# Expert products in plain float32, token-major outputs and expert jobs of two batches, in a two-layer kernel on one core

## The chip, the cores and the metric

The kernel runs on one core of a Trainium2 chip. The metric is device time in microseconds (us) from launch to the last store; lower is better. The core has TensorE (PE: matrix products and 128x128 transposes, results to PSUM), VectorE (DVE), ScalarE (ACT), GpSimd (POOL) and SyncE (SP, which here only issues DMAs). Each engine runs its own instruction list in order. Engines wait for each other through semaphores, so an instruction whose input is late holds up everything behind it on its engine.

## The reference, cut to what matters

The input has 8 batches of 1024 tokens of 128 features, in float32. Four layers follow each other, each on the layer-normalised rows, each added to its input:

```
A: k, q, v = x@Wk, x@Wq, x@Wv ; decay = clip(f(tanh(x@cs1)@cs2))       # linear attention
   state_t = state_{t-1}*decay_t + k_t v_t ; y_t = q_t . state_t ; y @ Wo
B: top 2 of 8 experts, weights renormalised, width 352:
   y = sum_e cw_e * ( silu(x@W1_e) * (x@W3_e) ) @ W2_e
C: conv over 3 tokens, silu, state-space scan with 16 states over t,
   gated by silu(x@Wz), @ Wout + bout
D: top 2 of 8 experts, width 128, and 2 shared experts of width 128 on every token
```

A and C scan over the tokens of a batch. B and D work on rows gathered by expert.

## The kernel before, in words

Letters A to D name the layers as above, `T` = 1024, `HW` = 512 (half a batch), `P` = 128.

**Layer A**, per batch: PE turns the normalised rows (`s_turn`), ACT copies them out of PSUM as float32 and again as float16 (L1115, L1117), DVE makes the remainder as a second float16 (`a_lo`, L1340). For each of 16 steps (8 features by 2 halves) PE makes the value product in three float16 passes (`a_value`, through `product`, L835 to L837), DVE multiplies with k (L1377), scans (L1366), multiplies with q (L1384), and PE adds up through `Wo` with the weights stationary and 512 columns moving (`a_sum`, L885). The result is feature-major: ACT copies it (L1139), PE turns it back (`transpose_out`, L860), DVE adds it to x (L1345).

**Layer C**, per batch: products for u, z, dt and the B and C rows; these rows go to DRAM and come back broadcast to 128 partitions (`c_brow`, `c_crow`, 512 KB each). For each of 16 states ACT makes exp (L1173), DVE multiplies, scans and multiplies (L1435, L1440, L1426), and PE adds up 1024 columns (`c_sum`, L927). Then `c_out` (L937), a copy with the bias on ACT (L1177), transposes, and the addition.

**Layers B and D** go by jobs. A job is one layer of one batch, 16 jobs in all. `prepare` normalises the rows, turns them for the gate's product, chooses the experts (`m_choose`), ranks (`m_rank`) and places them (`m_place`), then POOL scatters the rows to DRAM with indirect DMAs (L796, 16 per job) in blocks of rows of one expert. Rows are held as two float16 parts (L1111, L1331). A job has 12 blocks of 256 rows, each half of 128 rows with its own expert: 192 blocks. Per block SP loads the up weights (`b_w13`), the down weights (`b_w2`) and the rows (`b_rows`). PE turns both parts (L973), ACT copies them (L1202), PE makes the up products in three float16 passes each (L835 to L837: 12 products of 128x128 in a B block, 4 in a D block), ACT makes silu (L1207, L1214), DVE gates (L1540, L1551), PE makes the down product with the weights stationary (L998), so its result is feature-major; ACT copies it to `y_ring` (L1223), PE turns it (L1007), ACT scales it by the gate into `yrow` (L1231), and SP stores it. When a job's blocks are stored POOL gathers the outputs back and adds them to x (L813, 16 indirect DMAs per batch and layer). The shared experts of D run at the head of the D job, also in three float16 passes, with a copy and transposes of the output.

The float16 parts of the expert weights are made on the chip at the start: maxima (`peak`, L1269), a power-of-two scale (`scale`), the split on ACT and DVE (L1074, L1289), and a store to DRAM (`keep`).

The order of all steps is a string, `ORDER`. Each letter takes the next step of one chain (the dictionary `chain`). Every engine goes through the same list and carries out its own part of each step, so the string fixes the order on every engine, on SP's and POOL's queues too.

Of the kernel before, what the change touches and what calls it, by code (L numbers as in the profile page):

```python
# [6 lines left out]
BF16 = mybir.dt.bfloat16  # L7
F16 = mybir.dt.float16
# [6 lines left out]
P = 128  # L15
# [27 lines left out]
class BankUses:  # L43
# [32 lines left out]
    "CWAAAWAAWWAAWAAWAAAPAAAAAAAAAAAAAAAAAAAAosAokqAswokqsAkqwoswqkAwosAokqAswokqAswokqAswokqAswoqAswoqAswoqAswoq"  # L76
    "AswoqAswoqAWWwWWWWWsoqswCqCAwwCAwwwAAPAAPAAAPPAPPAPPAAAPAPAPPAAPPAAPAAAAAPAAPKoPAsqkowesPKAqkwoesAPokqAswokP"
    "qAswokqAswPokqAswokqAPswokqAswoPqAswoqAswPoqAswoqAswoqAswoqARAwRRRRRsAoqAwsqTwwMwwAUwTPAALPUAPVUKAALAAVMNAAe"
    "PTAAAPULUAAVUKMAAYPAALPVAAOZUPAASALRNPePoTYUPMAVPosskAqUKkqOZwoLUPVPAsTSwoRkLUPANeMYOZPSRVUKqLUVwLoUPNeTYMOV"
    "UZPTKsALMskUoSkLqARPswqkqwowVPsANeokqAsYUPowkVAqUKswToPqLUALVwsMNeoqAYsPOZwoUSqAsRwoqAPVwoUKsTLAMVUsNLPqeUoY"  # L80
    "OZqAAwSwRsAVUKTLMqUAVwLoUsNeVUqYOZwKTwLUVMwAwSNwRPAeAYAOPAALPAPAUAAAPVAAUKATALZVUMAASLUARAVOZAANeAAUYALROZVU"
    "oSTLKNsMqkAYPSowPesARPqkUoPwPVUKsALqkUowLVAsNeokqAYswoUkqTAsMwoOZVUKAkLqUoTLsOAZSwMqSGkoRwRsAVkqNeoswAsUYoOZ"
    "VUKAsLUoTLqMASqwRoGwqsAwsqowqGAswoqAswoqGswVqUPPVAGwwNePPwwUwAYTPKOZGMLUSRLPVGAAUPNeYAVUTGCLUKMALAAAAAPAPVAA"
    "AAAAAAAAAAANeCAAYPUOZCoCVUKTAsCPoCqSsCRwCkqCMkLPVCCCPCACCowsCCPqkCCACCNeCoCYsPPAUqkwoLUsAVkwoUKsALCCVkoUCqAs"
    "LCwCoOUqAqwsbbwoTcVAcsZUKkkNMCLTUdSVqRewqxYwbxMdboOZhALSURsNedoqAswoYdOqAswZSOZoRqASVwRoUKsTLUsAqMVLwqUowpyc"
# [12 lines left out]
    "cbxUPPGNVbPeUdTYPMyKLOUGZLRSPAVAPNeUYAPhAOAVUKpTZAMPxyLAVSAUxcNeLhPdUAVRUbhYTbLUKPAOhMZASARVGLAAAAUdpNeVUxYT"
    "AOMcApLbUKhALyZcVASAURxdNeGVUTYALKhOUAZVbMyPpRLSAcpAUdNeAAGVUYKTdoOyZsLqURAxcLSwGkVbMoUdsNeVUqkTYLUKhOAGwZMV"
    "SyoLRdpUscNeGVkUYqOZTxKALUowsARMVLSGyobkqsNekqUYOZhARwPSwVdoUKTsAoLUPqAswLVMqUkkoNeVPsUYOZTPKwLMAkUSLoGVAsUN"  # L100
    "eoVUsYOZKTAqPLUqMVwqRNPoRLsSwYeUpOZAVcURoKTLUqMVAsLUNeoVUqYOZsKTALwxMwVKqNohUYeOZwLRUsRdAeVUTqKwoMwpLAKsyVqN"
    "eoesUYLqbOZVUSRLpSwSVNccxUSGbhLNwVUYxLwwVUKwTLyMwVhOeNUKaNPxTyGpePyhKYLMPVcpGUKPPLVPyPTPMPGpPyPGOCNeUYPNLCKC"
    "GYCOZeCCNeCYOZRVURLaNKVGTYCMOCZUCNLRPYKOZVCPNSSYSOZTGSeCeRPMSTCRUKCPCMLCTVeUCMNLTPCYVMUOZPTCMRLSCVCUKPNLCYVU"
    "OZTCCSNLePCCVYCMCOUKCCZCCLVCCPOZSCSNCCPPbbccYCOZPSNdPPRRYRPPxORbxPPZbhSdRNPePhYTOZPMSGURdpdPcpLcxbxdbhUyPPVT"
    "dPUKMyLPGUTLMPVGxUbPNeVUYOZGTKhMLULVSdNpeUpGYyVRchcOZUKTLUxGyMxRLVSdUbhbNeYVUTGdOpKZLUpyRhLcycMSGVdUxNeVUhYT"
    "LUKOPxMVLbUZhbRNdeVUPTGLpSKpyYVMPUdOcycxLUbxPbhZRNeVUYPThdOKLUpScpyPLVcMUxZRNVdexUTPLUhSbybLKVYUMhOZPSNPdeYO"
    "ZVUKPTLpUpyLPVSMcUxdcNVRbUhKYTLyxUMVRLUheNeVUYTLOpKMZVUxNLKpUYOZVUTRLhSMyccKVULNVKUYLOZVUeLKOZVULpNSpNSSGVUY"
    "eTNLMRVURRNPKOyaPePeyPLePYVeUPPNKTMyPLGVPeCKUPKCPGCCPTCCMCLTGMOYNeCYOZCaSNCGRPeYVUKPOZLOCZTMNVSURPYCCOSCeRCK"
    "CPLCVUTLCKMVZSPCCRCCPNeCCYUCCLVCCPOZTCCNeMCCYURCCLSPVTCOZCCSNRPbbccMCYTUKPMdTPOZMSNLGxxbYOZVbUhSdNRGepyLRhcY"
    "dVpPUcxTdNGPyMbxLbhUTPVpPchyLMYdpPcxUPbOxZPVUKPNPhyLPPKYdVpSORPyPbhcZUSdNePLUPRYOZTSdORVUKMLUxpTbLMVcyxZRdbh"  # L110
    "USGNeVdUpTYLUKOhyZMRNVLexdUxPSVcUYKPOZTLUGNepLYVOZUchbNMePVUYdOhTSyRbKMpGLUycLVRZpUSSdNVexPUTYyLhKUMVOPZbxcL"
    "URNRpdSVUcTKhyGLUeYVLOUbMZVUKTdGNxpLUehyRbLcMVGSYUpdOVUKTyxZLhNbPeUMVYLUSxOZcVUKTPLNMVhUYNSLeUpYePOZVUcyLxKV"
    "OZhUKLUPNVUpYSOZSeyLVSPPeNKUYLpOZKPVULVNGSUPeLeNVURYRLRORVNGRaRNPyTYCMCPTCMUKCTCCMPLVUPeCCLOCKNaPYCOZePPSTVU"
    "CRNMPGLTKYGMOVUZCPCeSRNKPCLPGVUCKTCPCLCKYGMNCCeYCeVeCOZGCCSOUCKCLVZCCNCCPeYGCSCPRCCRNCTYCCOGbbccMCGZUKdOTZMe"
    "LTPRxSSMVURLTxbdNVbUPhMYTLOhPZSMNVpdUKpTPyMxLxccYhdObPybVUZhSLNePYVUKLNdVpYcpydPcxdOybZxSbhNYPOZPdSNeYOZpOSZ"
    "GchySxdRpbPRcxyRGbPPhRRRPPhdPPpdcxyGPPbpTMcPyxTUMbGhPLhdUVUKGLPUpTMxycLVbPpUNeGVPUdTPLycKUMYLGOZRPSVxUNePGYO"
    "ZbVUTKLMVUxNLPehUYOZbVUTKLVdpNPcUhRMyLRehUPSdSVUKTpMPLUcxybxLVYdOpUPVUKTyhLUcZVMRPNheLUYNpSeVUYPTxLOcyZKVMhO"
    "ZURLURNpPeVUYTLOSMyVZSKUpGNLSUYeOZVUKTLyMVNCRSCYRCCeUCGCLCCUCOZCSRCPCCVUTKPCPCCLUCVMCLCCCCUCCVUKCCLVCCNCCKCC"
    "YCCeTCUMCNCeebbccLUCYdOVUKTLxMKVULxZdNhbbKVdUpYdRcOhLyeeZpeOZVUcLRxRNdVSSNxbUSGYhbLOyadVNhUKTNMPpcxyPexbPLbh"
    "GYPPVdpUKhPyLGpcTPxycMbPdOVUKaNGhPLexYdOVbUPKhTGZPNpeYLNcPySPRMGeYTOZMROSZSdRPVGxdbpUKPNLyGYTcOZVUepMNLSTYcV"  # L120
    "UMxOKZTyMhPLbNeYVUOZhSLRNdSPRVURpKYLxNyPcpbYdKTVOyhcMPZKxTUMNdhTYbMOePZLOpeSxycZdSVbhUSPKNYLOpKxyZPdVhcUbNSY"
# [11 lines left out]
def build(nc, t, out):  # L133
# [1494 lines left out]
```

## Time and profile before

| what | value |
|---|---|
| median of 3 runs | 1948.63 us (1947.36 to 1950.04) |
| profiled execution: span from first to last instruction | 1960.7 us (the page gives no other time for it) |
| busy: PE / DVE / ACT / POOL | 76% / 72% / 59% / 51% of the span |
| mean granted TensorE clock | 0.890 of full speed |
| DMA | 393.00 MB, mean 200 GB/s |

Busy time is time in which an engine carried out an instruction that the profiler records. A float32 matmul shows as two instructions. Idle time is put down to what ended it; "issue" is idle time that ended with nothing that the profile shows.

### The profile page before, as it was taken

To read this page: it belongs to the slowest core of one execution; us is meant where nothing else is said; L and a number is where in the kernel's file an instruction comes from. 1 tells how busy PE (TensorE), PEld (TensorE's weight loads), DVE (VectorE), ACT (ScalarE), POOL (GpSimd) and SP (SyncE) were. 2 spreads that over 40 slices of the span, in tenths; PEclk is the share of its full clock that TensorE was granted. 3 is DMA by queue.
4 is the path that set the end of the run, shared out by engine and by line. 5 is a ranking of instruction groups with operands and counts; after the bars stand their busy time and mean duration, and the time that the engine had idled before them with its cause. 6 is when DMAs were issued, how large, how long until landed. Compare 5 with 4: busy or idle time off the path is not lost.

```text
span 1960.7 us, 32118 instructions
## 1 busy us (share of the span) xinstructions
PE 1485.2 (76%) x9858; PEld 950.1 (48%) x9858; DVE 1404.1 (72%) x2696; ACT 1155.1 (59%) x2075; POOL 999.0 (51%) x711
## 2 busy tenths in 40 slices
PE   0767988889997778769887788789768778766761
PEld 0223655555662446656554555466536544433540
DVE  3777869699988886678856774886688399398410
ACT  2232453577466544867357755985866697674550
POOL 0024335602728364748274826356888258655465
PEclk9979999999998798889997988799889899878895
DMA  8931545478928654979657985897789588487563
GB/s 261 136 96 58 146 138 126 108 242 279 271 87 239 188 149 116 295 250 292 191 135 230 284 288 130 264 327 240 199 273 317 173 252 272 110 284 210 135 162 66
DMA packets 343140, 393.00 MB, mean 200 GB/s; under 512 B 37784, under 2 KB 280504, under 8 KB 342712
## 3 DMA queue, kind: packets, MB, share of 16 engines
q1 hardware_dynamic: 297912, 357.23, 59.9%
q0 software_dynamic: 45056, 33.72, 9.6%
q8 instruction: 79, 1.29, 0.3%
q14 instruction: 93, 0.76, 0.1%
HBM read 333.10 MB, written 59.69 MB: 200 GB/s over the span
## 4 chain that ended last, share of the span: by engine, by line
PE 25%; issue 20%; POOL 19%; DVE 15%; ACT 10%; DMA 7%; SPq 3%; POOLq 0%; DVEq 0%; ACTq 0%; another core or an unknown queue 0%
POOL x L813 6%; POOL rows_D L796 6%; POOL rows_B L796 4%; PE bank L998 4%; PE bank L927 3%; DVE arena_a L1366 3%; PE bank L835 2%; PE bank L837 2%; PE bank L836 2%; POOL xrow L794 2%; DVE arena_c L1440 2%; DMA mix<-weights_B 2%; DVE arena_a L1384 2%; PE bank L871 2%; PE bank L885 2%
## 5 line engine op out<-in xcount | busy, mean ns | idle before, releaser
L813 POOL DMA_INDIRECT x<-outs,slot_idx x256 | 501.3, 1958 | 379.2 <-DMA outs<-yrow 301.4
L835 PE MATMUL bank<-xT_ring,mix 128*128 128x128 f16 (+1 forms) x1536 | 296.9, 228 | 57.1 <-DMA mix<-weights_B 17.3
L927 PE MATMUL bank<-arena_c,ident 128*128 128x512 f32 x512 | 285.5, 688 | 47.2 <-DVE arena_c L1426 46.8
L836 PE MATMUL bank<-xT_ring,mix 128*128 128x128 f16 (+1 forms) x1536 | 296.3, 228 | 0.0
L837 PE MATMUL bank<-xT_ring,mix 128*128 128x128 f16 (+1 forms) x1536 | 296.1, 228 | 0.0
L1440 DVE TENSOR_TENSOR_SCAN arena_c<-arena_c 128x1024 f32<-128x1024 f32 x128 | 291.0, 2281 | 3.6 <-ACT arena_c L1173 3.3
L998 PE MATMUL bank<-mix 128*128 128x128 f32 (+1 forms) x1536 | 231.5, 297 | 54.2 <-issue 22.5
L998 PEld LDWEIGHTS bank<-mix 128*128 128x128 f32 (+1 forms) x1536 | 206.4, 206 | 88.7 <-issue 84.2
L796 POOL DMA_INDIRECT rows_D<-xrow,slot_idx x128 | 208.4, 1628 | 74.8 <-POOL xrow L794 35.5
L835 PEld LDWEIGHTS bank<-xT_ring,mix 128*128 128x128 f16 (+1 forms) x1536 | 169.2, 110 | 108.6 <-issue 55.9
L1551 DVE SCALAR_TENSOR_TENSOR mix<-bank,winv,mix 96x256 f32<-96x256 f32 (+1 forms) x192 | 91.4, 476 | 178.6 <-ACT mix L1214 106.1
L796 POOL DMA_INDIRECT rows_B<-xrow,slot_idx x128 | 160.9, 1257 | 76.1 <-POOL xrow L794 35.5
L836 PEld LDWEIGHTS bank<-xT_ring,mix 128*128 128x128 f16 (+1 forms) x1536 | 167.8, 109 | 36.2 <-issue 31.4
L1231 ACT ACTIVATE yrow<-bank,xg 128x128 f32<-128x128 f32 x384 | 120.0, 364 | 107.2 <-PE bank L1007 77.5
L927 PEld LDWEIGHTS bank<-arena_c,ident 128*128 128x128 f32 x512 | 101.1, 216 | 147.3 <-issue 83.0
L837 PEld LDWEIGHTS bank<-xT_ring,mix 128*128 128x128 f16 (+1 forms) x1536 | 168.0, 109 | 0.1
L1426 DVE TENSOR_TENSOR arena_c<-arena_c 128x1024 f32<-128x1024 f32 x128 | 154.5, 1214 | 12.3 <-DMA arena_c<-bc_rows 12.0
L1435 DVE TENSOR_TENSOR arena_c<-arena_c 128x1024 f32<-128x1024 f32 x128 | 154.2, 1214 | 12.7 <-DMA arena_c<-bc_rows 9.4
L1173 ACT ACTIVATE arena_c<-arena_c,A_w 128x1024 f32<-128x1024 f32 x128 | 145.6, 1148 | 27.0 <-DVE arena_c L1440 26.1
L885 PE MATMUL bank<-arena_a,Wo 128*128 128x512 f32 x256 | 140.2, 639 | 27.3 <-DVE arena_a L1384 26.5
L1223 ACT COPY y_ring<-bank 128x256 f32<-128x256 f32 x192 | 71.1, 370 | 144.7 <-PE bank L998 134.4
L1214 ACT ACTIVATE mix<-bank,winv 96x256 f32<-96x256 f32 (+1 forms) x192 | 91.0, 474 | 80.9 <-PE bank L837 65.4
(219 smaller groups left out, 2882.0 us busy)
## 6 DMA issues: line engine op xcount, KB each, us to landing
arena_c<-bc_rows SPq DMA_DIRECT2D x256, 512.0 KB
mix<-weights_B SPq DMA_DIRECT2D x192, 352.0 KB
mix<-weights_B SPq DMA_DIRECT2D x192, 192.0 KB
outs<-yrow SPq DMA_DIRECT2D x192, 128.0 KB
mix<-weights_D SPq DMA_DIRECT2D x192, 128.0 KB
xg<-rows_B SPq DMA_DIRECT2D x96, 129.0 KB
xg<-rows_D SPq DMA_DIRECT2D x96, 129.0 KB
mix<-weights_D SPq DMA_DIRECT2D x192, 64.0 KB
```

What stands on the lines that cost most here:

```text
L796: pool.indirect_dma_start(out=xs_d[s, b % 2], out_offset=bass.IndirectOffsetOnAxis(ap=slot_idx[:, q % RJ, c, j:j + 1], axis=0), in_=xrow[: ...
L813: pool.indirect_dma_start(out=x[:, b % XS, j, :], out_offset=None, in_=y_d[q], in_offset=bass.IndirectOffsetOnAxis(ap=slot_idx[:, q % RJ, ...
L835: pe.matmul(o, hi, xh, start=True, stop=False)
L836: pe.matmul(o, hi, xl, start=False, stop=False)
L837: return pe.matmul(o, lo, xh, start=False, stop=True)
L885: filled(added_up(b, k), pe.matmul(bank[A_BANKS[1]][:], Wo[:, f, :], qs[:, k % RQ, :], start=(f == 0), stop=(f == EF - 1)))
L927: last = pe.matmul(bank[C_BANKS[h]][:], ident[:], half(hb[:, n % RR, :], h), start=(n == 0), stop=(n == NS - 1))
L998: last = pe.matmul(o[:, j * P:(j + 1) * P], w2(q, k, j)[0:rows, c, :], h_ring[n % RH][0:rows, at:at + P], start=(c == 0), stop=(c == NC[s] ...
L1173: act.activation(dA[:, n % RDA, :], dt, ACT.Exp, scale=A_sb[:, n:n + 1]).then_inc(c_dA.sem, 1)
L1426: dve.tensor_tensor(hb[:, n % RR, :], hb[:, n % RR, :], Cb[:, g % RB, :], ALU.mult).then_inc(c_prod.sem, 1)
L1435: dve.tensor_tensor(hb[:, n % RR, :], Bb[:, g % RB, :], w, ALU.mult).then_inc(c_dBx.sem, 1)
L1440: dve.tensor_tensor_scan(hb[:, n % RR, :], dA[:, n % RDA, :], hb[:, n % RR, :], 0.0, ALU.mult, ALU.add).then_inc(c_scan.sem, 1)
```

## The change

1. **Numbers.** The splitting of weights and rows into float16 parts is gone, with `peak`, `scale`, `split`, `keep`, `a_lo`, `m_hi`, `m_rows`, `m_lo`. Rows and weights stay float32, and each product is one float32 matmul in place of three float16 ones. The expert weights are copied DRAM to DRAM at the start.
2. **Token-major outputs.** The down product, the shared down product, `a_sum` and `c_out` take the activations as the stationary operand and the weights as the moving one, 128 columns each. The transposes of outputs and the copies ahead of them are gone (`b_out`, `b_down_read`, `a_end`, `s_end`, `c_out_read`, `sh_out`, `sh_read`); the bias of `c_out` comes from a matmul with one row.
3. **Jobs of two batches.** 9 jobs: B01 B23 D01 B45 D23 B67 D45 D6 D7. A job of two batches has 20 blocks, one of a single batch 12, so there are 164 blocks. A job's choice and placing runs once for both batches. The scatters become a chain of their own (`X`), as do the shared experts (`u`, `l`, `v`, `n`). A gather waits for the gathers of the job before.
4. **Residence.** x has 8 places rather than 7; `xn` is gone, the rows are normalised right into `xrow`; the statistics are kept by parity of the batch.
5. **`ORDER`** is a new string of 4840 letters (before 5769).

```diff
-            def product(o, hi, lo, xh, xl):
-                pe.matmul(o, hi, xh, start=True, stop=False)
-                pe.matmul(o, hi, xl, start=False, stop=False)
-                return pe.matmul(o, lo, xh, start=False, stop=True)
...
-    JOBS = [(j[0], int(j[1])) for j in "B0 B1 B2 D0 B3 B4 D1 B5 D2 B6 D3 B7 D4 D5 D6 D7".split()]
+    JOBS = [(j[0], [int(b) for b in j[1:]]) for j in "B01 B23 D01 B45 D23 B67 D45 D6 D7".split()]
+    BLOCKS = [-(-((2 * T * len(own) + E * (P - 1)) // P) // NBT) for _, own in JOBS]
...
             def a_value(b, k):
-                filled(f"A{b}.v{k}", product(o, Wv[0][:, c], Wv[1][:, c], half(xA_hi, h), half(xA_lo, h)))
+                filled(f"A{b}.v{k}", pe.matmul(fill(f"A{b}.v{k}"), Wv[:, f, :], half(normA, h), start=True, stop=True))
             def a_sum(b, k):
-                filled(added_up(b, k), pe.matmul(bank[A_BANKS[1]][:], Wo[:, f, :], qs[:, k % RQ, :],
-                                                 start=(f == 0), stop=(f == EF - 1)))
+                for j in range(TH):
+                    rows = slice(j * P, (j + 1) * P)
+                    last = pe.matmul(bank[A_BANKS[1]][:, rows], qs[:, k % RQ, rows], Wo[:, f, :], start=(f == 0 and j == 0),
+                                     stop=(f == EF - 1 and j == TH - 1))
...
             def c_out(b, h):
-                filled(n, pe.matmul(fill(n), Wout[:], half(w, h), start=True, stop=True))
+                for j in range(TH):
+                    rows = slice(j * P, (j + 1) * P)
+                    pe.matmul(o[:, rows], ones[0:1, :], bout_row[:], start=True, stop=False)
+                    last = pe.matmul(o[:, rows], half(w, h)[:, rows], Wout[:], start=False, stop=True)
...
             def rows_turned(q, k):
-                for part in range(2):
-                    for i in range(NBT):
-                        c = part * NB + i * P
-                        last = pe.transpose(o[:, c:c + P], xg16[:, m % RX, i, part * D:(part + 1) * D], identh[:])
+                for i in range(NBT):
+                    last = pe.transpose(o[:, i * P:(i + 1) * P], xg[:, m % RX, i, 0:D], ident[:])
             def up_products(q, k, name, parts):
-                        last = product(o[:, i * NB + j * P:i * NB + (j + 1) * P], wd[:, v, f], wd[:, v + 1, f],
-                                       xT_ring[:, m % 2, 0, rows], xT_ring[:, m % 2, 1, rows])
+                        last = pe.matmul(o[:, i * NB + j * P:i * NB + (j + 1) * P], wd[:, v, f], xT_ring[:, m % 2, rows],
+                                         start=True, stop=True)
             def down_product(q, k):
-                        last = pe.matmul(o[:, j * P:(j + 1) * P], w2(q, k, j)[0:rows, c, :], h_ring[n % RH][0:rows, at:at + P],
+                        last = pe.matmul(o[:, j * P:(j + 1) * P], h_ring[n % RH][0:rows, at:at + P], w2(q, k, j)[0:rows, c, :],
                                          start=(c == 0), stop=(c == NC[s] - 1))
-            def outs_turned(q, k):
...
-            def outs_moved(q, k):
...
+            def m_gather(q, i, c, first):
+                s, b = JOBS[q][0], JOBS[q][1][i]
+                if c == 0 and first == 0:
+                    if i == 0:
+                        for r in range(RY):
+                            m = max(m for m in range(block_no[q, BLOCKS[q] - 1] + 1) if m % RY == r)
+                            wt.wait_ge(y_out[r], 16 * (m // RY + 1))
+                    if q:
+                        job_gathered(wt, q - 1)
```

## Rows read from the trace of the kernel before

**Rows 1.** The page: busy time, share of the span and instructions of each engine.

```profile
PE 1485.2 (76%) x9858; PEld 950.1 (48%) x9858; DVE 1404.1 (72%) x2696; ACT 1155.1 (59%) x2075; POOL 999.0 (51%) x711
```

**Rows 2.** The page: shares of the span in the chain that ended last.

```profile
PE 25%; issue 20%; POOL 19%; DVE 15%; ACT 10%; DMA 7%; SPq 3%; POOLq 0%; DVEq 0%; ACTq 0%; another core or an unknown queue 0%
```

**Rows 3.** Busy us by stage: window, length, PE, PEld, DVE, ACT, POOL, clock, DMA share.

```profile
426.00:544.00 118.00, 108.03 (x843) 73.17 (x842) 112.43 (x132) 73.87 (x132) 50.22 (x17) 0.97 0.87 268
1684.00:1821.00 137.00, 95.67 (x456) 53.49 (x454) 102.03 (x163) 92.01 (x145) 81.07 (x49) 0.84 0.70 206
```

**Rows 4.** Timeline of PE, full clock: start us, us, line, operation, count.

```profile
556.25 0.60 PE L946 MATMUL bank<-ident,xn 128*128 128x128 f32 x4
565.51 1.02 PE L902 MATMUL bank<-arena_c,Wconv 128*128 128x512 f32 x2
567.23 0.22 PE L835 MATMUL bank<-xT_ring,mix 128*128 128x128 f16 x1
567.28 0.22 PE L836 MATMUL bank<-xT_ring,mix 128*128 128x128 f16 x1
568.81 1.50 PE L998 MATMUL bank<-mix 128*128 128x128 f32 x12
570.15 0.22 PE L835 MATMUL bank<-xT_ring,mix 128*128 128x128 f16 x1
```

**Rows 5.** Costliest groups of ACT: busy us, mean ns, idle before, releaser.

```profile
L1231 ACT ACTIVATE yrow<-bank,xg 128x128 f32<-128x128 f32 x384 | 120.0, 364 | 107.2 <-PE bank L1007 77.5 <-PE bank L837 12.1 <-remote 5.3
L1202 ACT COPY xT_ring<-bank 128x512 f16<-128x512 f16 x192 | 111.5, 581 | 41.8 <-PE bank L973 36.6 <-remote 2.6 <-PE bank L1007 1.4
L1173 ACT ACT_TABLE_LOAD x80 | 102.6, 1283 | 1.5
L1223 ACT COPY y_ring<-bank 128x256 f32<-128x256 f32 x192 | 71.1, 370 | 144.7 <-PE bank L998 134.4 <-issue 8.6 <-PE bank L1042 0.7
L1139 ACT COPY arena_a<-bank 128x512 f32<-128x512 f32 x16 | 9.4, 586 | 74.8 <-PE bank L885 74.2 <-issue 0.5
L1111 ACT CAST xrow<-xn 128x1024 f16<-128x1024 f32 x16 | 16.9, 1054 | 0.0
```

**Rows 6.** Groups of DVE.

```profile
L1440 DVE TENSOR_TENSOR_SCAN arena_c<-arena_c 128x1024 f32<-128x1024 f32 x128 | 291.0, 2281 | 3.6 <-ACT arena_c L1173 3.3
L1540 DVE SCALAR_TENSOR_TENSOR mix<-bank,winv,mix 128x512 f32<-128x512 f32 x96 | 71.2, 742 | 55.8 <-PE bank L837 38.2 <-issue 4.9 <-ACT mix L1207 4.8
L1331 DVE TENSOR_TENSOR xrow<-xn,xrow 128x1024 f16<-128x1024 f32 x16 | 19.4, 1216 | 14.0 <-ACT xrow L1111 12.2 <-issue 1.8
```

**Rows 7.** The waits: who waited for whom, us in total, times, longest.

```profile
PE bank L853 <- DVE Wv_lo L1289: 42.8, 1, 42.8
PE bank L1007 <- ACT y_ring L1223: 36.6, 41, 5.2
PE bank L998 <- ACT yrow L1231: 20.6, 28, 2.1
PE bank L1007 <- ACT yrow L1231: 12.5, 8, 6.6
```

**Rows 8.** Timeline at the start, and the first statistics of layer C.

```profile
23.70 0.20 ACT L1067 ACTIVATE tanh_base<-cols 128x1 f32<-128x1 f32 x1 [13.07 <-DMA cols<-in_bbc]
50.40 3.59 PE L871 MATMUL bank<-arena_a,cs_w 128*32 128x512 f32 x4 [5.71 <-POOL before L765]
354.80 1.64 DVE L1310 BATCH_NORM_STATS2 stats_C<-x 128x6 f32<-128x128 f32 x8 [3.95 <-DMA x<-outs,slot_idx]
```

**Rows 9.** Timeline of POOL in the last job: scatters from the first row, then gathers.

```profile
1850.45 1.08 POOL L796 DMA_INDIRECT rows_D<-xrow,slot_idx  x1 [0.83 <-POOL xrow L789]
1876.73 1.61 POOL L813 DMA_INDIRECT x<-outs,slot_idx  x1 [0.30 <-issue]
1950.77 1.56 POOL L813 DMA_INDIRECT x<-outs,slot_idx  x1 [0.30 <-issue]
1952.63 1.56 POOL L813 DMA_INDIRECT x<-outs,slot_idx  x1 [0.30 <-issue]
```

More of the change, by code:

```diff
@@ L81 @@
[L81 to L85, printed above, removed]
@@ L402, in attention, with blocks, shared @@
+        def blocks(name):
+            return [(name, q, k) for q in range(len(JOBS)) for k in range(BLOCKS[q])]
+        def shared(name, n):
+            return [(name, b, i) for s, own in JOBS if s == "D" for b in own for i in range(n)]
         def attention(b):
             steps = [(n, "A", b, h) for n in ("s_turn", "s_turned") for h in range(NH)]
-            steps += [(m, b, "cs", h) for m in ("a_in", "a_read") for h in range(NH)] + [("a_lo", b)]
+            steps += [(m, b, "cs", h) for m in ("a_in", "a_read") for h in range(NH)]
@@ new lines, in m_rstd, with m_scatter @@
+            def m_rstd(q, i):
+                inverse_deviation(JOBS[q][0], JOBS[q][1][i])
+            def m_scatter(q, c, first):
+                s = JOBS[q][0]
+                if c == 0 and first == 0:
+                    wt.wait_ge(s_zeroed[s, NTH[q] % ROW_SETS[s]], 16)
+                    wt.wait_ge(placed, q + 1)
+                    all_scattered(wt, q - 1)
+                    pool.tensor_copy(xrow[:, 0:JT[q], D], gate12[:, q % RJ, 0, 0:JT[q]]).then_inc(row_gate, 1)
+                    wt.wait_ge(row_gate, q + sum(JT[:q]) + 1)
+                for j in range(first, first + 2):
@@ L854, in s_turn @@
                 filled(n, last)
-            def transpose_out(s, b, h):
-                U.wait_empty(wt, f"{s}{b}.o{h}")
-                o = fill(f"{s}{b}.outT{h}")
-                for j in range(TH):
-                    last = pe.transpose(o[:, j * P:(j + 1) * P], OUT[s][:, h, j * P:(j + 1) * P], ident[:])
-                filled(f"{s}{b}.outT{h}", last)
             def a_in(b, name, h):
@@ L919, in c_bc @@
                 U.wait_empty(wt, f"C{b}.u{h}")
-                filled(n, pe.matmul(fill(n, rows=BC), Wbc[:, 0:BC], half(xs, h), start=True, stop=True))
+                filled(n, pe.matmul(fill(n, rows=BC), Wbc[:], half(xs, h), start=True, stop=True))
             def c_sum(b, n):
@@ L955, in m_logits @@
                                      start=True, stop=True)
-                filled(f"lg{q}", last)
+                filled(f"lg{q}.{i}", last)
             def m_rank(q):
@@ L1124, in a_in @@
                 if name == "k":
-                    read(n, act.activation(half(kT, h), psum(n), ACT.Copy, scale=down["Wv"]))
+                    read(n, act.copy(half(kT, h), psum(n)))
                 if name == "q":
```

868 lines of the change are left out of this document (354 added, 514 removed).

## The prediction

> **What bounds the kernel now.** I read the page's busy times first, then the chain, then the stages, then the rows of what changes. No engine is full: PE 76%, DVE 72%, ACT 59%, POOL 51% [rows 1]. The chain that ended last is spread in the same way: PE 25%, "issue" 20%, POOL 19%, DVE 15%, ACT 10%, DMA 7% [rows 2]. The reader is to see that nothing here is worth its busy time. Engines alternate, in an order written out by hand, and the span is 475 us longer than PE's busy time. The stages differ [rows 3]: from 426 to 544 PE is busy 108 and DVE 112 of 118 us, so there both are full; from 1684 to 1821, the last scan layer beside a D job, DVE has 102 of 137 us, ACT 92, POOL 81, and the handovers between them fill the rest.
>
> **The change part by part, on PE.** Prices are distances between starts at full clock [rows 4]. Float16 passes start 0.05 to 0.06 us apart; I take 0.056, so a product of three costs 0.168 (512 columns: four times as much, 0.67). Six float32 products of 128 columns, each with its own stationary operand, take 1.34 (568.81 to 570.15), so 0.223 each. A single pass of 0.22 has 0.16 of tail, so a float32 product of 512 columns in 1.02 costs 0.86, and four float32 transposes in 0.60 are 0.11 each.
> - Up products: 96 B blocks of 12 and 96 D blocks of 4 are 1536 at 0.168, 258 us. Afterwards 80 of 12 and 84 of 4, 1296 at 0.223, 289 us: +31.
> - Value and shared up products: 192 of 512 columns, 0.67 to 0.86: +36.
> - Down products: 768 to 648 (6 or 2 per block) at 0.223: -26. `a_sum` and shared down: 160 times 0.86 become 160 times 4 x 0.223: +5. `c_out`: 16 times 0.86 become 16 times 8 x 0.223 with the bias: +15. The one-row bias product stands in no row; it lies between nothing and a full 0.223, and I take the full price.
> - Output transposes, 384 for blocks and 192 others at 0.11: -63. Turns of block rows: 768 at 0.056 become 328 at 0.11: -7.
>
> PE in all: -9 us, so nothing. "Plain float32" doesn't relieve PE; what it gains in fewer blocks and turns it gives back at 0.223 against 0.168.
>
> One rule of the Trainium skill speaks against these edits. The row above shows six different stationary operands in 1.34 us, so their loads stay behind the streaming. The page "TensorE: Matmul & The Clock Gate" (Weight-path perf modes) says that the fast way of loading weights is open to types other than FP32 only; every product of the new kernel would lose it. If a slower load showed at each product the PE sum would turn clearly positive; by the row it adds nothing, and I go by the row.
>
> From rows alone, the bound of the new `a_sum`, whose stationary operand DVE has only just written: below, its four parts cost the 0.86 of now; above, they can't hide their loads behind each other and cost as much as four half-filled 0.60 groups would allow, 4 x 0.38 (0.223 and one tail of 0.16), +0.66 each, 106 us in all. I take 0.223, since the down product has the same form.
>
> **On ACT** [rows 5]. The `y_ring` copies go: -71. The turned rows are 256 float32 columns instead of 512 float16 ones, at the 0.370 of the copy of that shape, 164 times: 111.5 to 61, -51. Casts and half-batch copies that only served the parts and the feature-major outputs go, 17 us (L1111) and some 80 half-batch copies at 0.586, 47 us: -64. Fewer blocks: `yrow` 120 to 103, -17, and 44 silus fewer, at the 0.37 to 0.59 of copies of their shapes, -20. Weight splits -10. Table loads: walking through both order strings and counting the changes between exp, ln and the silu/tanh group on ACT gives 207 before (the trace shows 204) and 173 afterwards, -34 at 1.283: -44. Sum -277 of 1155.
>
> **On DVE** [rows 6]. The three remainders (32 of 1.216) -39. The gates keep their price (the form without a scalar lies between nothing and the 0.742 of now); 16 wide ones and 28 of half the width fewer, -12 for the first and up to as much again for the others: -25. Maxima and splits at the start -20. Choice and placing run 9 times with wider rows, not 16 times: about -25, between nothing and half of their cost. Sum -109 of 1404. The scans (128 of 2.281) stay.
>
> **POOL** keeps its 256 gathers and 256 scatters: 0. **DMA**: 28 of 192 blocks go, 15% of what blocks load and store; the two 512 KB broadcasts per state stay.
>
> **What of it reaches the end.** An engine's saving counts in the share of its busy time that lies on the chain: ACT 10% of 1960.7 is 196 of 1155, 0.17, so -47; DVE 294 of 1404, 0.21, so -23; PE 0.33 of 9, -3; DMA 137 on the chain, half of it blocks' loads, 15% of that: -10. Output turns: PE stood 37 + 21 + 12 = 70 us for the `y_ring` and `yrow` copies [rows 7]; two handovers per block go, but other work shares these gaps, so half, -35. The start: PE waited 42.8 us for the low part of Wv [rows 7] and made its first product at 50.4 [rows 8]. The last small loads are in at 23.7 [rows 8]; normalising and turning needs some 7 more, so 31: -20. The DRAM to DRAM weight copies are hidden by the 150 us of layer A before any expert block; without that cover they cost some tens of us once.
>
> Against this stands the pairing. Sixteen scatter DMAs take 26.3 us (1850.45 to 1876.73), gathers 1.86 each [rows 9]. A pair puts 32 in a row, 53 us, ahead of 20 blocks, and its second batch waits for all of it. At the start the first pair can't begin before batch 1 has left layer A, so C's first statistics stay near 355 [rows 8] in spite of the earlier start. Where the string has other DVE work at hand this costs nothing; for the seven pairs I take +30, between 0 and 7 x 26 = 182. The new wait of a gather for the job before holds POOL's scatters behind it, but POOL does these in order anyway; it is within the 30.
>
> Sum: -47 - 23 - 3 - 10 - 35 - 20 + 30 = -108. The span of 1960.7 becomes 1853. The runs' median lies 12 below the profiled span, so the time is 1841.
>
> **Rivals.**
> 1. PE sets the pace and ACT's and DVE's relief turns into their idle time. For it: PE is first in busy time and on the chain, 108 of 118 us where things are dense, and its work falls by only 9. Against: the last third, where PE has 96 of 137. Only the start and PE's own share come off, 20 and 10 at the clock of now: span 1931, time 1919.
> 2. Slower: lumps on POOL. A pair's 32 scatters, 20 blocks and 32 gathers stand in one piece between two layers, and the scan layers of the next batches run dry. In the string, between the statistics of C4 and C5 stand 44 gather DMAs and 30 scatter DMAs, 44 x 1.86 + 30 x 1.64 = 131 us of POOL at its best, beside some 91 us of DVE; between the same marks the old string has 24 and 32, 97 us, beside some 120 of DVE. It decides from the point where the work in hand is shorter than the 53 us scatter. Each pair then pays 26: 182 in place of the 30, sum +44, span 2005, time 1993. Against: the letters of DVE work between a pair's preparation and its gathers are some 200 us for the later pairs.
>
> **How the numbers follow.** Forecast 0.58, rival 1 0.23, rival 2 0.17; 0.02 for a draw by other ways. The forecast's own range: without lumps and with all 70 us of the turns -173, time 1776; with ACT's and DVE's shares halved and 60 for the lumps -43, time 1906. The range over all reaches below for a chain that gives back more of ACT than its share (some 30 us), 1745, and above to between the rivals, 1960. A measurement tells 0.2%, 4 us, from no change. Faster 0.80 (the forecast and rival 1), same 0.03, slower 0.17.
>
> **What would show it.** ACT near 880 busy, DVE near 1295, PE within 30 of 1485, POOL near 1000. The first product of layer A near 31; the first statistics of C near 355. Float32 products 0.22 apart in the up products and in the new `a_sum`; if 0.38, the load isn't hidden. No idle PE behind copies of outputs. If PE's share rises above 80% with little gain, rival 1; if POOL's share of the chain grows well over 19% and DVE waits for gathers, rival 2. The forecast is wrong if the time is above 1906 or below 1776.

## The result and the profile after

The kernel after takes 2002.57 us (1998.39 to 2009.84, 4 runs), the kernel before beside it 1948.18: ratio 1.027 [1.024 to 1.030], slower by 54 us. The forecast was 1841. Its profiled span is 2003.1 us at a mean granted clock of 0.863 of full speed; before it was 1960.7 at 0.890.

The kernel after, the page: busy time, share of the span and instructions.

```profile
PE 1528.4 (76%) x7536; PEld 1041.4 (52%) x7536; DVE 1302.6 (65%) x2413; ACT 886.6 (44%) x1623; POOL 884.7 (44%) x702
```

Against [rows 1] ACT lost 268 us and DVE 101, PE gained 43, POOL's recorded time fell by 114. ACT's and DVE's work is what was forecast (880 and 1295). PE's isn't (within 30 of 1485 was forecast), nor POOL's (near 1000): POOL has as many scatters and gathers as before, but each is shorter (gathers 1.79 us in place of 1.96, scatters 1.21 in place of 1.44 on average). None of ACT's and DVE's relief is to be seen in the span, which means that it became idle time. PE's idle time is 475 us before and after.

The chain of the profile after breaks off (its engines' shares add up to 11%), so its shares can't be set against [rows 2]; groups, waits and marks have to do. Groups of the kernel after: busy us, mean ns | idle before, releaser.

```profile
L917 PE MATMUL bank<-xT_ring,mix 128*128 128x128 f32 x1952 | 287.5, 300 | 43.6 <-ACT xT_ring L1086 21.7 <-DVE mix L1385 7.0 <-DMA mix<-weights_D 6.2
L859 PE MATMUL bank<-arena_c,ident 128*128 128x512 f32 x512 | 290.1, 702 | 104.3 <-DVE arena_c L1256 104.2
L819 PE MATMUL bank<-Wo,arena_a 128*128 128x128 f32 x1024 | 152.4, 297 | 52.8 <-DVE arena_a L1215 51.5 <-DVE x L1176 1.2
L1106 ACT ACTIVATE yrow<-bank,xg 128x128 f32<-128x128 f32 x328 | 102.1, 363 | 187.0 <-PE bank L930 186.3
L1086 ACT COPY xT_ring<-bank 128x256 f32<-128x256 f32 x164 | 60.3, 368 | 167.3 <-PE bank L905 103.2
```

`yrow` costs 102.1 and the turned rows 60.3, as counted from [rows 5] (103 and 61). What has grown is PE's waiting: 104.2 us for DVE in the sums of layer C (L859) and 51.5 in those of layer A (L819), where the kernel before had 46.8 and 26.5. The timeline of PE (start us, us, line, operation, count):

```profile
10.62 3.08 PE L794 MATMUL bank<-ident,arena_a 128*128 128x128 f32 x8 [10.62 <-POOL blk_no L716]
13.78 3.59 PE L805 MATMUL bank<-arena_a,cs_w 128*32 128x512 f32 x4
256.31 0.41 PE L905 MATMUL bank<-ident,xg 128*128 128x128 f32 x2
541.18 1.95 PE L917 MATMUL bank<-xT_ring,mix 128*128 128x128 f32 x16
550.14 1.13 PE L819 MATMUL bank<-Wo,arena_a 128*128 128x128 f32 x8 [0.36 <-DVE arena_a L1215]
```

Layer A's first product starts at 13.78, not at 50.40 as in [rows 8]: 37 us earlier, where 20 were counted. Eight float32 up products (16 instructions) take 1.95 us and four in the new `a_sum` 1.13. Less the tail of 0.16 that is 0.22 and 0.24 apart; [rows 4] gave 0.22. But no block is worked on before 256.31, and the first statistics of C come at 408.28, where [rows 8] has 354.80:

```profile
408.28 1.64 DVE L1154 BATCH_NORM_STATS2 row_sums<-x 128x6 f32<-128x128 f32 x8
```

So after 37 us of lead at the start the kernel is 53 us behind one fifth of the way, and 42 at the end of the profiled spans (54 by the medians: the profiled execution before was a long one, 12 above its median).

### The profile page after: what moved, and what is told of

Read it like the earlier page. It is cut to its first block and busy times, and to the rows that moved or that the text cites. A ratio compares the mean times of both kernels' runs of the same rounds, so it can differ in the third digit from the quotient of the medians.

```text
span 2003.1 us, 25885 instructions
## 1 busy us (share of the span) xinstructions
PE 1528.4 (76%) x7536; PEld 1041.4 (52%) x7536; DVE 1302.6 (65%) x2413; ACT 886.6 (44%) x1623; POOL 884.7 (44%) x702
## 5 line engine op out<-in xcount | busy, mean ns | idle before, releaser
L917 PE MATMUL bank<-xT_ring,mix 128*128 128x128 f32 (+1 forms) x2592 | 366.7, 295 | 58.1 <-ACT xT_ring L1086 21.7
L917 PEld LDWEIGHTS bank<-xT_ring,mix 128*128 128x128 f32 (+1 forms) x2592 | 340.6, 202 | 100.8 <-issue 64.8
L859 PE MATMUL bank<-arena_c,ident 128*128 128x512 f32 x512 | 290.1, 702 | 104.3 <-DVE arena_c L1256 104.2
L859 PEld LDWEIGHTS bank<-arena_c,ident 128*128 128x128 f32 x512 | 104.6, 223 | 227.2 <-DVE arena_c L1256 133.7
L819 PEld LDWEIGHTS bank<-Wo,arena_a 128*128 128x128 f32 x1024 | 136.7, 206 | 114.6 <-DVE arena_a L1215 93.1
L1385 DVE TENSOR_TENSOR mix<-bank,mix 128x256 f32<-128x256 f32 (+1 forms) x164 | 68.1, 419 | 194.9 <-ACT mix L1098 192.2
L819 PE MATMUL bank<-Wo,arena_a 128*128 128x128 f32 x1024 | 152.4, 297 | 52.8 <-DVE arena_a L1215 51.5
L740 POOL DMA_INDIRECT rows_D<-xrow,slot_idx x128 | 155.3, 1214 | 74.0 <-POOL xrow L738 47.9
L1106 ACT ACTIVATE yrow<-bank,xg 128x128 f32<-128x128 f32 x328 | 102.1, 363 | 187.0 <-PE bank L930 186.3
L810 PE MATMUL bank<-arena_a,Wv 128*128 128x512 f32 x256 | 144.9, 650 | 29.7 <-DVE arena_a L1208 29.7
L1086 ACT COPY xT_ring<-bank 128x256 f32<-128x256 f32 x164 | 60.3, 368 | 167.3 <-PE bank L905 103.2
L1208 DVE TENSOR_TENSOR arena_a<-bank,arena_a 128x512 f32<-128x512 f32 x128 | 87.5, 684 | 49.0 <-PE bank L810 38.9
L905 PE MATMUL bank<-ident,xg 128*128 128x128 f32 x328 | 71.2, 303 | 58.6 <-DMA xg<-rows_D 37.4
```

The source lines that it names most:

```text
L740: pool.indirect_dma_start(out=xs_d[s, NTH[q] % ROW_SETS[s]], out_offset=bass.IndirectOffsetOnAxis(ap=slot_idx[:, q % RJ, c, j:j + 1], axis=0),
L810: filled(f"A{b}.v{k}", pe.matmul(fill(f"A{b}.v{k}"), Wv[:, f, :], half(normA, h), start=True, stop=True))
L819: last = pe.matmul(bank[A_BANKS[1]][:, rows], qs[:, k % RQ, rows], Wo[:, f, :], start=(f == 0 and j == 0), stop=(f == EF - 1 and j == TH - 1))
L859: last = pe.matmul(bank[C_BANKS[h]][:], ident[:], half(hb[:, n % RR, :], h), start=(n == 0), stop=(n == NS - 1))
L917: last = pe.matmul(o[:, i * NB + j * P:i * NB + (j + 1) * P], wd[:, v, f], xT_ring[:, m % 2, rows], start=True, stop=True)
L1106: ins = act.activation(yrow[:, m % RY, i, :], o[:, i * P:(i + 1) * P], ACT.Copy, scale=xg[:, m % RX, i, D:D + 1])
```

## The experiments

Each run is called by the first part of its label. In each the kernel before, the kernel after or an earlier experiment is changed in one thing, or in the few that the text names. Times are medians; a ratio is to the kernel before on the same chip.

**Single jobs in the old order.** The kernel after with 16 jobs of one batch, its order that of the kernel before with the vanished steps left out:

```
-    RX = 5
+    RX = 6
-    JOBS = ... "B01 B23 D01 B45 D23 B67 D45 D6 D7"
+    JOBS = ... "B0 B1 B2 D0 B3 B4 D1 B5 D2 B6 D3 B7 D4 D5 D6 D7"
```

> The changed kernel's numbers and layout (float32 products, token-major outputs, x resident) with 16 jobs of one batch (192 blocks) and the order of steps of the kernel before, less the steps that are gone; six places for block rows as before. Theory 1 (the loss comes from the jobs of two batches and their order, ahead of numbers and layout): the ACT and start savings now show, 1870 to 1925 us, faster than before. Theory 2 (the float32 products are the loss, PE sets the pace with more work per block): 1990 to 2040, since this kernel has 17% more blocks than the changed one at 0.223 a product. First statistics of layer C near 335 in theory 1.

1969.7 us, ratio 1.011 [1.009 to 1.013]: in neither theory's range. One flaw: the old order begins with a wait of ACT and DVE for the weights of C, which here are loaded late, so that the first statistics came at 51.14. The start's gain was thereby left out, and more: the first product of layer A starts at 59.41, 9 us later than in the kernel before [rows 8].

> The single-job float32 kernel of e1_single with one step moved: the wait of DVE and ACT for the C weights stands ahead of the convolution's weights (as in the kernel after) instead of at the head of the order. Nothing else differs. In e1_single the first A statistics start at 51.1 us, in the kernel after at 5.0. Theory 1 (the start is on the path at full price, pairing and the new order are what costs after its gain): the first A product comes about 28 us earlier, the kernel takes 1942 (1930 to 1950), a little under before, and the kernel after stands 60 over it. Theory 2 (the start's gain is given back at the first C stage, since what stands behind it waits for weight tables, x loads or the experts): within 10 us of e1_single's 1970, and pairs with the new order cost some 33.

1915.6 us, ratio 0.983 [0.978 to 0.987]: faster than both kernels, and 54 less than `e1_single`. The first product starts at 14.08, 45 us before that of e1 and 36 before that of the kernel before. In e4 the mark of the first C statistics is

```profile
308.82 1.65 DVE L1158 BATCH_NORM_STATS2 row_sums<-x 128x6 f32<-128x128 f32 x8 [4.69 <-DMA x<-outs,slot_idx]
```

46 us ahead of [rows 8], and its span (1913.8) ends 47 ahead of the kernel before's; by the medians it is 34. Neither range is met, but the result lies beyond theory 1's, on the side away from theory 2: moving one wait brought at least the 45 us by which it moved the start. Against the kernel before, e4 gains about what its start gains (36), so that all the other changes together, without pairs, come out near nothing.

**Output turns alone.** The kernel before with the down products of blocks and shared experts token-major, float16 parts, single jobs and order kept:

```
-  pe.matmul(o[:, j * P:(j + 1) * P], w2(q, k, j)[0:rows, c, :], h_ring[...][0:rows, at:at + P], ...)
+  pe.matmul(o[:, j * P:(j + 1) * P], h_ring[...][0:rows, at:at + P], w2(q, k, j)[0:rows, c, :], ...)
-  b_out, b_out_read, sh_out and y_ring
```

> The kernel before with one part of the change alone: the down products of blocks and of the shared experts take the activations as the stationary operand, so the output copies and transposes of blocks go (192 ACT copies of 0.37, 384 PE transposes of 0.11). Float16 passes, single-batch jobs and order kept. Theory 1: 1885 to 1925 us, 35 to 60 gained from 70 us of PE waits. Theory 2 says the same here, but that it beats the float32 version of the same order (e1_single) by 60 or more; theory 1 says the two lie within 30 of each other.

1941.3 us, ratio 0.998 [0.996 to 1.000]. ACT's busy time fell by 66 and PE's by 49, and the time by some 5 us. That is a miss of both theories' 35 to 60. The two versions of the old order lie 28 apart (e1) or, with e1's start mended, 26 the other way (e4), so the float16 passes aren't faster by 60 either.

**What work costs when it is added.** Up products issued twice; ACT's two block copies issued twice; three quarters of `a_qs` twice:

```
+  repeat(wt, lambda: act.copy(again[:, 0:NB], o))                                        (e5)
+  repeat(wt, lambda: dve.tensor_tensor(again[:], half(qT, k // EF)[:, 0:384], S[...], ALU.mult))   (e6)
```

> The changed kernel with every block up product issued twice (the second overwrites the first with the same numbers): 1296 more float32 products of 0.223, 289 us of PE work. Theory 2 (PE sets the pace): +200 to +290 us. Theory 1 (PE waits for others in most stages): +80 to +180, as part of it falls into PE's idle 475 us.

> The kernel after with ScalarE's copies of the block turns and of the down products issued twice (the extra ones into a spare tile): 164 x 0.37 + 328 x 0.36 = +179 us of ScalarE, in front of what TensorE waits for. The prediction gave a microsecond of ScalarE 0.17 us of the end: +30, so 2033. Theory 1 (ScalarE at 44% has slack almost everywhere, what it was relieved of brought nothing): +0 to +15, so 2003 to 2018. Theory 2 (the turn copies are links of the chain through TensorE, each waits on them): +80 or more, 2083 and up; then the ScalarE relief must have been worth much, and something as large ate it.

> The kernel after with three quarters of each product of q and state of the attention computed a second time on VectorE (128 extra products of 128x384 into a spare tile, some 0.5 us each = +64 us of VectorE, in stage A). The prediction gave a microsecond of VectorE 0.21 us: +13, 2016. Theory 1 (VectorE holds TensorE in the A and C stages, L859 waits 104 us for it, L819 51.5): a weight of 0.5 or more, +32 and up. Theory 2 (VectorE is as slack as ScalarE): under +10.

2174.6, 2050.7 and 2044.7 us. Busy time by the pages of e3, e5 and e6:

```profile
PE 1764.4 (81%) x10128; PEld 1302.7 (60%) x10128; DVE 1306.9 (60%) x2413; ACT 887.8 (41%) x1623; POOL 886.4 (41%) x702
```

```profile
PE 1547.7 (75%) x7536; PEld 1052.3 (51%) x7536; DVE 1303.8 (63%) x2413; ACT 1009.5 (49%) x2115; POOL 883.4 (43%) x702
```

```profile
PE 1535.1 (75%) x7536; PEld 1048.4 (51%) x7536; DVE 1360.2 (67%) x2541; ACT 886.7 (43%) x1623; POOL 887.7 (43%) x702
```

A microsecond of added busy time costs 172/236 = 0.73 on PE, 48/123 = 0.39 on ACT and 42/58 = 0.73 on DVE. The prediction had 0.33, 0.17 and 0.21. In e6 PE's wait for DVE in `a_sum` grew from 51.5 to 85.0 us. In e3 theory 1 holds (+172, inside 80 to 180); in e5 neither theory's range was met, 48 lies between them; in e6 the first holds. These prices are by busy time, which falls a little for the other work when the mean clock rises (0.863 to 0.897 in e3); by the 289 us of products that e3 adds at 0.223 each, its price is 0.60.

**Fewer blocks without pairs.** `e4_single_late_c` with ten blocks a job:

```
-  for k in range(BLOCKS[q])
+  for k in range(10)
```

> e4_single_late_c (16 single jobs of 12 blocks) with ten blocks in each job: 160 blocks in place of 192, the order the same but for the steps of blocks 10 and 11 of each job, which are left out (rows of an expert layer that lie in those blocks are left uncomputed and count as zero; one more transfer a job writes the zeros). It gives what pairing was to bring, fewer part-filled blocks (164 in the kernel after), without pairing. A block holds TensorE some 3.9 us in e4 (440.7 + 222.0 + 83.9 us over 192), so 32 of them 125 us. Theory 1 (a microsecond of TensorE's work is worth 0.6, as e3_double_up gave): -75, so 1841 (1830 to 1860), which is where the prediction had the kernel after; then pairing and its order cost 160 together. Theory 2 (the blocks fill time in which TensorE waits for the mixers anyway): -30 or less, 1885 and up, and pairing costs 115.

1869.9 us, ratio 0.960 [0.956 to 0.964], 46 less than e4, between the two theories. PE's busy time fell by 82 us (to 1485.8), not by 125: the sum had added groups that run into each other, and the mean clock fell too (0.896 to 0.878). So 0.56 for each microsecond. The kernel leaves out the rows that would lie in the last two blocks, so it measures a time and is no replacement. This kernel has 160 blocks (the kernel after 164), float32, token-major outputs, the early start, and no pairs. It stands 133 us under the kernel after.

**The first pair undone.** The kernel after with B0 and B1 as single jobs, and e4's order up to the first statistics of C1; the ring of six places is tried by itself in e10:

```
-    JOBS = ... "B01 B23 D01 B45 D23 B67 D45 D6 D7"
+    JOBS = ... "B0 B1 B23 D01 B45 D23 B67 D45 D6 D7"
```

> The kernel after with the first pair undone: jobs B0, B1, then B23, D01 and on as before; up to the first statistics of C1 the order is that of e4_single_late_c (with B3 prepared behind B2), from there that of the kernel after; the ring of block rows has six places. 168 blocks in place of 164. Theory 1 (the opening: with B01 no product of a block stands beside A1, A2 and most of A3, and C0 waits for all twenty blocks; after stood 64 us behind e4 at C1): C1 starts within 15 us of e4's 511, and of the 64 us most is kept to the end: 1940 (1930 to 1960). Theory 2 (each pair pays for its own lumps, 8 to 12 us in each of seven): 1985 or more, with C1 early and the lead given back before the end.

> The kernel after with six places in the ring of block rows in place of five, as e4 and e9 have. Theory 1 (the ring is no limit): 2003 within 6. Theory 2 (rows fetched late hold TensorE, 37.4 us at L905, and the place more takes half of it): 1985.

1981.9 and 2008.2 us: the ring brings nothing (theory 1 of e10), the first pair costs 21 (26 against e10). e9 lies between its two ranges, close to theory 2's. C1 starts at 545 in place of 575 and most of that lead is kept (the profiled span ends 25 earlier), but it isn't e4's 511. Nearly half of the rest is a stall that the timelines of e9 show, first SyncE's queue, then PE:

```profile
86.03 32.40 SPq L600 DMA_DIRECT2D rows_D<-zero_rows  x3
119.56 18.31 SPq L638 DMA_DIRECT2D mix<-weights_B  x2
142.90 5.18 SPq L656 DMA_DIRECT2D xg<-rows_B  x6
```

```profile
134.43 2.08 PE L820 MATMUL bank<-Wo,arena_a 128*128 128x128 f32 x8 [3.26 <-DVE arena_a L1216]
151.31 0.69 PE L906 MATMUL bank<-ident,xg 128*128 128x128 f32 x2 [14.80 <-DMA xg<-rows_B]
```

Pairs need row sets of 20 blocks, and zeroing three of them holds the queue ahead of the first block's weights and rows.

> e9_two_single_first (1981.9) with the zeroing of the three row sets of D issued at the first D preparation in place of the queue's start. In e9 these three transfers held the queue 32.4 us (86 to 119), and the first weights and rows of B0 came late: TensorE and VectorE stood still from 136 to 151. Theory 1 (that stall is a start cost like any other, kept to the end): B1's statistics at 140 in place of 154, and 1967. Theory 2 (later stages take it back, or the transfers collide later): 1978 or more.

> e4_single_late_c (1915.6) with the five row sets of the experts as long as pairs need them (20 blocks of 256 rows in place of 12): only their zeroing at the queue's start grows, from 7.9 to 13.2 MB, that of the three D sets from 16 to 32 us of the queue. Theory 1 (part of the price of pairs is this zeroing, since B0's weights and rows stand behind it, as the stall of 15 us in e9 showed): +12 to +20, 1928 to 1936. Theory 2 (the lead is regained later): under +5.

1994.1 us with the zeroing moved: B1's statistics came at 139.3 as expected, but the stretch between the first statistics of A5 and A6 became 32 us longer (240 before, 272 then): the zeroing stands in the queue there, and PE waits 29.4 us once for block rows behind it. Theory 1 fell, theory 2 holds. And 1931.3 for single jobs with long sets: +16, theory 1. So the longer sets cost 16 us in an order whose blocks start early. In the kernel after, the zeroing is through at 121 us and the first expert weights are asked for only at 180, so there it holds up nothing that the trace shows.

**Scatters.** The second half of each job's scatters left out, in pairs and in singles:

```
                     if c:
-                        wt.wait_ge(scattered_first[j], ...)
-                        pool.tensor_copy(xrow[:, j, D:D + 1], gate12[...]) ...
+                        continue
```

> The kernel after without the second half of the scatters (the rows of each token's second expert are not written, so their slots hold zeros; every product and transfer of the blocks stays): a pair issues 16 scatters in place of 32. In the trace of after 32 scatters lie between a pair's table and its first rows, 58 to 88 us, and the first turn of rows comes 64 to 96 us behind the table; the second half takes some 2.1 us each with its gate copy, 34 us a pair. Theory 1 (the prediction's second rival: the blocks of a pair wait for its scatters, and little else is there for TensorE): of 7 x 34 + 2 x 17 = 270 us less waiting a third or more reaches the end, 1915 or less. Theory 2 (the scatters lie beside the blocks before; the order alone costs): 1980 or more.

> The same cut in e4_single_late_c (1915.6): a single job issues 8 scatters in place of 16, 17 us each time, 16 x 17 = 270 us in all, as in e11. Theory 1 (in single jobs the blocks of the job before cover the scatters): a gain of 10 to 30, 1886 to 1906, well under that of e11. Theory 2 (GpSimd's work is on the path in both alike): the same gain in both.

1954.9 and 1871.3 us: 48 less in pairs and 44 less in singles, 0.21 for each microsecond of the 231 and 211 that POOL was relieved of. For e12 theory 2 holds; e11 lies between its ranges (1915 or less, 1980 or more), so its idea that the scatters are hidden fell too. The scatters cost, but alike, so they don't explain the distance between pairs and singles.

**PE work in C's sums.** One product of zeros more per step:

```
+  if h and 0 < n < NS - 1:
+      last = pe.matmul(bank[C_BANKS[h]][:], zero_rows[:, 0:P], half(hb[:, n % RR, :], h), start=False, stop=False)
```

> The kernel after with one product of zeros more in each step of the C sums but the first and the last (112 products of 128x512 float32, 0.59 us each at the full clock, in place, adding nothing to the result): +66 us of TensorE, all in the stages in which it waits most for VectorE (L859, 104.2 us). Theory 1 (in after TensorE stands idle there and its clock falls, 0.80 over 1569 to 1706 us against 0.90 in e4's C6 stage; work there is hidden and holds the clock): between -15 and +10, 1988 to 2013. Theory 2 (TensorE's work is worth 0.6 everywhere, as with the up products): +40, 2043.

> The same 112 products of zeros in e4_single_late_c (1915.6), where blocks stand beside the C sums in nearly every stage and TensorE waits 57.7 us for VectorE. Theory 1 (the idle time of after is what differs): a larger cost than in after, +30 to +45, 1946 to 1960. Theory 2 (no difference): the same sum as in e14.

2047.5 and 1945.0 us: +45 in pairs and +29 in singles, for some 70 us of PE's busy time each (96 us of products: one takes 0.86, its two instructions together, where the expectation had 0.59). Theory 1 of both fell; for e14 theory 2 holds, for e15 neither does. Where PE waits most, its work cost more, though not by much beyond the noise (43 and 28 by the ratios, each within some 10). A likely reason, only argued: the waits for DVE there are links of the layer's own chain, products to scan to products, and with no block beside it a longer link lengthens the stage. The mean clock rose (0.863 to 0.884) and saved nothing that shows.

**Orders moved about.**

```
-ORDER = ...
+ORDER = ... (the same letters, moved)
```

> The kernel after with nothing changed but its order of steps: some 15,500 small moves of steps were tried, and those kept that shorten a reckoning of the five engines' queues with each step's duration as the traces have it (TensorE's clock left out). Theory 1 (the order written for the kernel after is what costs, not the pairs): a gain of 50 or more, 1953 or less, and the distance to single jobs treated the same way (e17) falls from 87 to under 40. Theory 2 (the pairs cost by what they need, two batches before the first block, row sets, mixer stages without blocks): a gain of 10 to 40, no more than e17's, and the distance stays near 87.

> e4_single_late_c (1915.6) with its order moved about in the same way and as many tries (14,100). Its order came from the kernel before, whose ScalarE and VectorE were busier by 124 and 72 us. Theory 1 (a fixed order hides what the relieved engines could give): 30 or more faster, 1885 or less. Theory 2 (the order was good already): within 10 of 1915.

2027.3 and 1947.2 us, 25 and 32 slower than what they started from, outside every range expected. The reckoning that chose the moves promised gains and the runs showed losses, so it can't say what a good order for pairs would take. All that it shows is that the distance between pairs and singles, treated alike, stays at 80.

## Why the prediction was wrong

The forecast missed by 162 us, and e8 cuts the miss in two, as near as 160 blocks stand for 164. Without the 30 for pairing the sum was 1811; single jobs with ten blocks take 1870: the savings were 59 too large. Pairing and its order cost 133 in place of 30: 103 more.

**Against this stands the pairing: +30.** This step failed most. The prediction saw that "the first pair can't begin before batch 1 has left layer A" and priced it at nothing, as C's first statistics would "stay near 355". They came at 408. Until 256 us PE has no block; a pair's 20 blocks must then all be done before C0. The step that failed is this one: pairing was charged for POOL's row of scatters and not for the stages of layer A that it leaves without a block beside them. In the first 400 us, window, length, PE, PEld, DVE, ACT, POOL, clock, DMA share, of after and then of e4:

```profile
100.00:200.00 100.00, 71.53 (x305) 40.98 (x304) 82.54 (x198) 16.28 (x45) 19.23 (x17) 0.88 0.62 97
300.00:400.00 100.00, 88.27 (x642) 74.46 (x641) 50.73 (x169) 38.06 (x95) 27.06 (x16) 0.93 0.67 189
```

```profile
100.00:200.00 100.00, 88.87 (x531) 67.16 (x530) 80.26 (x183) 31.37 (x77) 37.53 (x36) 0.97 0.45 124
300.00:400.00 100.00, 91.75 (x518) 65.92 (x519) 79.48 (x137) 57.71 (x109) 27.92 (x31) 0.95 0.59 180
```

The reader is to see two halves that hardly overlap: in after, layer A alone (DVE 83, PE 72), then blocks with little of layer A beside them (PE 88, DVE 51; 12 of the `a_sum` groups fall in that window). In e4 both stand side by side all along.

Much of the distance to single jobs is there by C1. The first statistics of C1 stand at 575 in after and 511 in e4, 64 apart; those of C7 at 1706 and 1637, 69 apart; the spans end 89 apart. So between C1 and C7 the pairs lose 5 us, with 28 blocks less to do. Against e8, with about as many blocks, the distance is 68 at C1, 98 at C7 and 123 at the end. Behind C7 one wait stands out in after, for the rows of the last job, with no block left to do beside its scatters: PE is busy 0.3 us from 1895 to 1922 (the longest such wait in e4 is 8.3 us).

```profile
1922.40 0.69 PE L905 MATMUL bank<-ident,xg 128*128 128x128 f32 x2 [27.13 <-DMA xg<-rows_D]
```

A stage in between shows the same thinness, but no loss. The last pair's table and the statistics of C6 stand at 1569; its rows are scattered and the first is turned 93 us later, and PE waits meanwhile for C's chain. Of after, first the timelines of DVE, POOL and PE, then PE's longest wait from 1569 to 1706 (us in total, times, longest):

```profile
1569.39 0.18 DVE L1365 CAST slot_idx<-pos 128x32 uint32<-128x32 f32 x1
1570.74 1.07 POOL L740 DMA_INDIRECT rows_D<-xrow,slot_idx  x1 [0.83 <-POOL xrow L733]
1656.98 2.18 POOL L740 DMA_INDIRECT rows_D<-xrow,slot_idx  x1 [0.78 <-POOL xrow L738]
1662.92 0.69 PE L905 MATMUL bank<-ident,xg 128*128 128x128 f32 x2 [9.18 <-DMA xg<-rows_D]
```

```profile
PE bank L859 <- DVE arena_c L1256: 33.1, 11, 16.8
```

In the same layer of e4 (1486 to 1637), whose last job's blocks are still at hand:

```profile
PE bank L863 <- DVE arena_c L1260: 7.3, 5, 2.6
```

and PE is busy 82% of that stage of e4, 62% of that of after (windows). But the stage takes 137 us in after and 151 in e4: it is thinner, not longer, since blocks that stand beside it in e4 are done elsewhere in after. So idle time in one stage doesn't give the price; the marks do. Over the whole kernel these waits are 57.6 us in e4 and 104.2 in after, those of `a_sum` for DVE 8.4 and 51.5, and the mean clock is 0.896 and 0.863. Shown is that the first pair costs 21 to 26 us (e9) with long row sets, and that about half of the distance is there by C1 (68 of 123 against e8). What the rest of the 133 owes to later pairs and what to this one order stays open: no run gave a second order for pairs that was as good as the one they have. That the lower clock is a part of it is only argued.

**What of it reaches the end: ACT -47, DVE -23.** Two things failed here. The weights were shares of the chain, and adding work costs two to three times as much as they say (e3, e5, e6). But taking work away isn't the reverse of adding it: e1 has 80 us more of PE than the kernel before, 189 less of ACT and 74 less of DVE. By the prices of added work that is 58 - 74 - 54 = -70; it is 21 slower, of which some 9 is its late start. e2 has 66 less of ACT and 49 less of PE and gains 5. So in these kept orders ACT's and DVE's relief gave nothing that shows, while every addition that was tried was paid. Rival 1 said that their relief turns into idle time, and that is borne out. That its number, 1919, is what single jobs took (1916) is luck: it was for the kernel with pairs, counted 20 for the start and 10 for PE, and e4 has a start of 36 and 82 us more of PE, not less.

**Handovers: -35.** Mis-sized. e2 takes out all `y_ring` copies and output turns of the blocks and brings some 5 us. [rows 7] had 70 us of PE waiting for those copies; other waits took their place: in e2 those for DVE in C's sums are 64.4 us (46.8 before), for the rows of D's blocks 31.2 (18.7), for DVE's counts in the ranking 27.4 (9.5), and the mean clock is 0.877.

**The start: -20.** Mis-sized the other way: the first product came 37 us earlier, and in e4, where nothing took it back, the kernel is 34 faster by the medians and 47 by the profiled spans. The prediction counted the step from 50.40 to 31, waiting for the last small loads; the new order asks for them later, so the first product stands at 13.78.

**PE: -9.** The price per product was right (0.22) for up, down and `a_sum` products, the sum wasn't: 1528.4 in place of 1476. One term was mis-sized, `c_out`, whose eight products per call were charged the full 0.223 each. At a granted clock of 1.00 they start 0.42 apart:

```profile
566.46 0.48 PE L872 MATMUL bank<-bout_row,ones 1*128 1x128 f32 x2
566.88 0.49 PE L873 MATMUL bank<-Wout_w,arena_c 128*128 128x128 f32 x2
567.29 0.48 PE L872 MATMUL bank<-bout_row,ones 1*128 1x128 f32 x2
```

That is 53 us for the 128 of them in place of 29, half of the miss, at the end of each C layer: DVE's idle time before it adds C's result to x is 50.3 us for these products, where the transposes of the kernel before held it 15.6. Part of the rest is the clock, 702 ns per instruction of the C sums in after and 690 in e4. The rule weighed there, of the Trainium skill's page "TensorE: Matmul & The Clock Gate" (Weight-path perf modes), that float32 has no fast loading of weights, didn't show as time in the other products: eight with their own stationary operands take 1.95 us. Whether it shows in `c_out`, or the change between one row and 128 rows does, no run here separates. The bound for `a_sum` (0.38 each) wasn't needed: four in 1.13.

**The rivals.** Rival 2's number, 1993, was nearly met, but hardly by its cause. It blamed POOL's row of 32 scatters, 26 us for each of seven pairs. That row is there (1570.74 to 1656.98), but halving it brings as much in single jobs (44) as in pairs (48). What pairs lack is the work that stands beside it in single jobs.

## What to carry to other kernels

Batching small jobs takes away padding and also the grain that fills the gaps of a latency-bound neighbour; before joining jobs, count for each stage of the neighbour what independent work would be left beside it, the first stage above all. Shares of the chain don't price a change in an order that is kept: adding cost 0.4 to 0.7 per busy microsecond of PE, ACT or DVE here and taking away 0 to 0.6, so price a saving by doing it alone. And a start that was made earlier was worth its full length here once nothing in the order waited again (e4): move the waits with it.

## What the runs showed that I had not expected

- One out-of-place wait at the head of two queues cost 54 us of 1970 (e1, e4).
- 5.3 MB of zeroing more at the queue's start cost 16 us (e18); in e13, moved into the middle, the zeroing of D's sets cost 12 us more than in e9.
- POOL's scatters are worth 0.21 us each microsecond in pairs and singles alike (e11, e12): in single jobs halving them was worth as much (44 us) as ten blocks in place of twelve (46).
- Added PE work cost 0.64 in stages in which PE waits long for DVE and 0.43 where it waits less (e14, e15), a difference little above the noise.
- A bias by a matmul with one row isn't free: it and the product after it start 0.42 us apart, where plain 128-row products are 0.22 apart.
- The best kernel of the study is `e4_single_late_c`: plain float32, token-major, x resident, 16 single jobs in the old order, 1915.6 us, ratio 0.983.
